# Summing the edge weights of an attention aggregation on VectorE instead of TensorE, in a two-layer graph network on one core

## The reference, cut to what matters

```
h = (x @ W1).reshape(N, 4, 512)
e = leaky_relu(as_n[src] + ad_n[dst], 0.2)          # one score per edge and head
ex = exp(e - segment_max(e, dst)[dst])
denom = segment_sum(ex, dst)                        # <- the sum that the change moves
alpha = ex / (denom[dst] + 1e-16)
out = segment_sum(alpha[:, :, None] * h[src], dst)  # 1250 x 4 x 512
h = elu(out + b1)
```

## Time and profile before

| | |
|---|---|
| median of 3 runs | 2060.86 us (2059.75 to 2064.29) |
| the profiled execution | 2063.02 us, its span 2061.2 us |
| the stage `aggregate_layer1`, first to last product | 1389 to 1719.6 us |
| PE busy, whole span | 1849.1 us, 90% |
| DVE busy, whole span | 1466.7 us, 71% |
| mean granted TensorE clock | 0.955 |

### The profile page before, as it was taken

One profiled execution on the slowest core, in us unless ns is written; L12 is line 12 of the kernel. 1 busy time (PEld: TensorE's weight loads), 2 busy tenths in 40 slices (PEclk: granted clock), 3 DMA queues, 4 the chain that ended last, 5 costly groups with the idle time before them and its releaser, 6 DMA issues. The chain is left out here.

```text
span 2061.2 us, 29930 instructions
## 1 busy us (share of the span) xinstructions
PE 1849.1 (90%) x11272; PEld 1758.3 (85%) x11272; DVE 1466.7 (71%) x2541; ACT 960.7 (47%) x1465; POOL 141.4 (7%) x129
## 2 busy tenths in 40 slices
PE   5998999993999999986999599969999995999898
PEld 4666779993999999985999479969999995999798
DVE  6887849996989988955555328728888885235666
ACT  1222222214888898864211222227788775232633
POOL 5000122110000000000110101200000000000000
PEclk9999999996999999997999799989999998999999
DMA  3111144435284445518543485454433404645402
GB/s 117 50 54 50 39 150 140 112 94 139 67 200 97 106 93 133 139 19 230 164 140 119 142 243 174 142 151 113 144 95 94 135 33 135 180 104 130 120 1 75
DMA packets 183967, 240.11 MB, mean 116 GB/s; under 512 B 76347, under 2 KB 155283, under 8 KB 183586
## 3 DMA queue, kind: packets, MB, share of 16 engines
q1 hardware_dynamic: 175852, 210.73, 37.2%
q0 software_dynamic: 7216, 24.91, 4.1%
q10 hardware_dynamic: 768, 2.70, 0.5%
HBM read 169.43 MB, written 68.86 MB: 116 GB/s over the span
## 5 line engine op out<-in xcount | busy, mean ns | idle before, releaser
L966 PE MATMUL p_o<-h_in,p 125*125 125x193 f32 x2400 | 399.1, 328 | 25.2 <-DVE p L925 20.9
L966 PEld LDWEIGHTS p_o<-h_in,p 125*125 125x125 f32 x2400 | 393.1, 188 | 28.2 <-DMA h_in<-h_rows 21.1
L882 ACT ACTIVATE e<-uv,col 125x1250 f32<-125x1250 f32 x240 | 299.2, 1346 | 18.1 <-DMA uv<-uv_rows 14.9
L1522 PE MATMUL p_o<-p_hi,h_parts 125*128 125x416 f32 (+1 forms) x960 | 282.5, 355 | 25.7 <-DVE p_lo L1456 19.4
L1522 PEld LDWEIGHTS p_o<-p_hi,h_parts 125*128 125x128 f32 x960 | 181.5, 189 | 31.9 <-issue 19.6
L920 DVE TENSOR_TENSOR e<-e 125x1250 f32<-125x1250 f32 x120 | 174.2, 1452 | 30.5 <-ACT e L882 30.4
L647 DVE CUSTOM_DVE_ANT_0 max_junk<-src_row,G 125x1250 bf16<-125x1250 f32 x120 | 180.9, 1574 | 10.6 <-DMA src_row<-score_rows 9.9
L734 PE MATMUL p_h<-pw_hi,x1T 128*125 128x384 f32 x720 | 186.0, 339 | 0.0
L925 DVE SCALAR_TENSOR_TENSOR p<-e,CT 125x1250 f32<-125x1250 f32 x120 | 175.3, 1461 | 4.1
L1259 PE MATMUL p_h<-pw_hi,x2T 128*125 128x256 f32 x960 | 175.8, 285 | 0.0
L1522 PE MATMUL p_o<-p_lo,h_parts 125*128 125x416 f32 (+1 forms) x480 | 169.7, 354 | 0.0
(11 more groups left out here) (236 smaller groups left out, 3469.1 us busy)
## 6 DMA issues: line engine op xcount, KB each, us to landing
f_raw<-turned SPq DMA_DIRECT2D x40, 500.0 KB
h_rows<-h_out SPq DMA_DIRECT2D x32, 560.0 KB
h_parts<-h_rows SPq DMA_DIRECT2D x40, 448.0 KB
uv<-uv_rows SPq DMA_DIRECT2D x24, 546.9 KB
turned<-out_f SPq DMA_DIRECT2D x18, 625.0 KB
G<-turned SPq DMA_DIRECT2D x20, 562.5 KB
h_rows<-h_out SPq DMA_DIRECT2D x24, 424.4 KB
h_in<-h_rows SPq DMA_DIRECT2D x24, 424.4 KB
```

The source lines that it names most:

```text
L882: last = a.activation(e[:, g % RING, kind, :], uv[:, hh, kind, :], ACT.Exp, bias=col_src[kind][:, bass.ds(i * 2 + hh, 1), s])
L966: last = nc.tensor.matmul(p_o[:, b, n * 256:n * 256 + C0 + 1], p[:, g % RING, d * T:(d + 1) * T], h_in[:, hh, s, 0:C0 + 1], start=(s == 0 ...
L1522: last = nc.tensor.matmul(p_o[:, bank(n, c), 0:w], h[:, s, kind, cols].bitcast(F32R), pp[:, g % RING, 0:w], start=(s == 0 and j == 0), sto ...
```

## The change

DVE adds the weights `p` of the ten steps of a third into one tile `acc` (two tiles of 418 columns, used in turn), nine additions for each third. The two products with ones in every step go. In their place PE makes one product for each third, of `ones_f` and `acc`, both plain fp32 rather than fp32r, after the second chunk of step 9; only this product needs the fifth bank. ACT no longer makes the rounded copy of `ones`. ACT's exponentials wait, beside `p_split`, for the addition that read the ring slot (`added`).

```
         p_lo = sb("p_lo", [T, RING, W], F32R)
         ones_f = sb("ones_f", [T, 128], F32)
-        ones = sb("ones", [T, 128], F32R)
+        acc = sb("acc", [T, 2, W], F32)
...
-            act.wait_ge(ones_set, 1)
-            a.activation(ones[:], ones_f[:], ACT.Copy).then_inc(ones_set, 1)
...
                 if g >= RING:
                     act.wait_ge(p_split, g - RING + 1)
+                    m, step = divmod(g - RING, NT)
+                    act.wait_ge(added, m * (NT - 1) + max(step, 1))
...
+            def add(n, s, low, before):
+                if s == 1 and n >= 2:
+                    dve.wait_ge(summed, n - 1)
+                if s > 1:
+                    dve.wait_ge(added, n * (NT - 1) + s - 1)
+                dve.wait_ge(p_ready, n * NT + s + 1)
+                v.tensor_tensor(acc[:, n % 2, 0:low.shape[1]], low, before, ALU.add).then_inc(added, 1)
+
             for g in range(STEPS_ALL):
...
                 v.scalar_tensor_tensor(low, low, 1.0, CT[:, s, at:at + w], ALU.min, ALU.mult).then_inc(p_ready, 1)
+                if s == 1:
+                    add(n, s, low, e[:, (g - 1) % RING, 0, 0:w])
+                elif s:
+                    add(n, s, low, acc[:, n % 2, 0:w])
                 if g:
                     rest_of_p(g - 1)
...
-            def sum_weights(g, n, s, w):
-                if s == 0:
-                    bank_is_free(n, CW)
-                for pp in (p_hi, p_lo):
-                    last = nc.tensor.matmul(p_o[:, bank(n, CW), 0:w], ones[:], pp[:, g % RING, 0:w],
-                                            start=(s == 0 and pp is p_hi), stop=(s == NT - 1 and pp is p_lo))
-                if s == NT - 1:
-                    last.then_inc(summed, 1)
-                return last
+            def sum_weights(n):
+                w = THIRDS[n % 3][1]
+                bank_is_free(n, CW)
+                pe.wait_ge(added, (n + 1) * (NT - 1))
+                nc.tensor.matmul(p_o[:, bank(n, CW), 0:w], ones_f[:], acc[:, n % 2, 0:w], start=True, stop=True).then_inc(summed, 1)
...
                 pe.wait_ge(p_split, g + 1)
-                if s:
-                    sum_weights(g, n, s, w)
                 for c in range(CW):
...
-                if s == 0:
-                    last = sum_weights(g, n, s, w)
+                    if s == NT - 1 and c == 1:
+                        sum_weights(n)
                 last.then_inc(p_used, 1)
```

More of the change, by code:

```diff
@@ L1312, in aggregate_layer1 @@
         p_used = sem("p_used")
+        added = sem("added")
         summed = sem("summed")
@@ L1486, in _ @@
         def _(pe):
-            pe.wait_ge(ones_set, 2)
+            pe.wait_ge(ones_set, 1)
             def bank_is_free(n, c):
```

## The result

The changed kernel takes 2098.09 us, the median of 4 runs (2091.59 to 2104.50), the kernel before 2062.57 (4 runs, 2059.75 to 2064.39). The ratio is 1.0173, with a 95% interval of 1.0139 to 1.0208: slower, clear of the noise. 2092 us was forecast, with 2084 to 2101.

The account below looks back on a forecast made before the run. The loop of DVE and ACT was taken as the bound, PE close behind. Paid additions +31 us, first end +1, last end -1: 2063.0 + 31 = 2094, less 2.2 for the median, 2092 us; range 2084 to 2101.

Parts of the forecast that it names:

- The bound: In each middle third, the loop of DVE and ACT sets the 27.53 us pace; PE is second, needing 26.7 us.
- Four free, five paid: Of nine additions a third, steps 4 to 7 hide in DVE's waits for ACT; five cost 3.1 us.
- The price of an addition: On DVE, each addition costs 0.62 us net, one dependence; bounds 0.51 and 0.73 us.
- The rule weighed: Skill's rule for DVE: every instruction waits for the pipe to empty, semaphores cost nothing extra; an addition would cost 0.51 us.
- Rival 2: On DVE, an addition costs the bare 0.51 us spacing: +25.5 us, 2086 us in all; chance 8%.
- The first end: Up to DVE's first taking of the sums, at 1416.4 instead of 1415.23: +1 us (0 to +2).
- The last end: From eleventh to last taking of the sums, where DVE waits for PE: 26.1 us against 26.97, so -1 us.
- this term of the sum: PE's one plain fp32 product of 416 columns per third costs 0.34 us, from the spacing of fp32 transposes.
- The upper bound: For the last third, with the lower clock and the fp32 product at 1.15 us: +0.2 us.
- rival 3: PE's clock stays at 1.2 GHz, 0.29 us a product, 35 us a third: +91 us, 2152 us; chance 3%.
- rival 4: PE paces the third and additions are hidden: 24.5 us a third, -36 us, 2025 us; chance 3%.
- The 2.2 us taken off for the median: Whole kernel: the median of the runs lies 2.2 us below the profiled execution, taking 2094 to 2092 us.

Follow-up runs that it names:

- e5: Changed kernel with all additions left out, PE's one product per third reading a tile of constant ones: 27.53 us a third, span 2059.9 us.
- e9: Kernel before with ACT's twelve ELU operations two to a step in steps 4 to 9: 27.0 us a third, median 2057.32 us, ratio 0.9980.
- e11: Changed kernel with all nine additions behind p_lo, one wait each, and ELU operations two to a step in steps 4 to 9: 28.51 us a third, 2076.04 us.
- e1: Changed kernel with only the additions of steps 4, 5, 6 and 7 of each third kept: 27.53 us a third, span 2059.1 us.
- e2: Changed kernel with only the additions of steps 1, 2, 3, 8 and 9 of each third kept: 31.01 us a third, span 2088.2 us.
- e4_onewait: Changed kernel with the additions of steps 2 to 9 waiting on one semaphore instead of two: 30.73 us a third.
- e3_late: Changed kernel with each addition placed behind the p_lo of its step instead of directly behind the weight: 30.04 us a third, 2088.5 us.
- e6: Kernel before with the nine additions put into DVE and PE's twenty products with ones kept: 30.9 to 31.3 us a third, span 2098.9 us.
- e7_pool: Changed kernel with the nine additions of a third made by GpSimd instead of VectorE: 30.5 to 30.8 us a third, ratio 1.0165 to the kernel before.

## Why the prediction was right, and where it was off

*The bound.* Right. The loop of DVE and ACT paces a third: e5 takes PE's cost away and gains nothing, e9 shortens DVE's waits for ACT from 3.3 to 1.4 us a third and gains 0.5 us until DVE waits for PE's sums; in e11 DVE has no wait left and a third is its bare need, 28.51 us. That need is 24.0 + 9 x 0.50: the 24.3 of the prediction was 0.3 too high, since a printed wait is some 0.09 us less than the whole gap (the maximum behind an ELU operation starts 0.65 us behind it after the wait is taken off, and 0.56 without a wait). The forecast's sum did not use it.

*Four free, five paid.* Right, and shown apart by e1 and e2.

*The price of an addition.* The step that was off. I took 0.62 us, one dependence; it was 0.69 to 0.70, since eight and, from the third third on, all nine of a third's additions wait on two semaphores. The surplus of 0.07 over five paid additions and ten thirds is 3.5 us of the 3.8 that the middle was too low. e4_onewait takes most of it away, 30.73 for 31.00. It lay inside the bound of 0.73, for a reason that I had not named. The text of the change showed both waits; I priced only the one that blocks.

*The rule weighed.* By the Trainium skill, VectorE: DVE Perf Modes, section The DRAIN you can't avoid, each instruction waits for the pipe to empty and a semaphore costs nothing extra; the section adds that an instruction that is not held starts earlier. Of the semaphore this kernel shows something else: 0.50, 0.63 and 0.70 us for one addition with no dependence ahead, with one, and with one and a second wait. Rival 2, built on it, would have been 30.08 us a third; the changed kernel has 31.00.

*The first end.* +2.0 instead of +1. DVE took the sums at 1417.22, 0.8 us later than the 1416.4 worked out. 0.6 is a later start of DVE (1386.56 against 1385.96), whose exponentials waited for a DMA; the ten second waits ahead of the first taking are worth up to 0.7, more than the rest; how much of that went into the early waits was not worked out.

*The last end.* +0.6 instead of -1. PE in the last third (timeline; then windows with PEclk behind POOL's busy time), which answers to the earlier trace rows:

```profile
1731.32 0.71 PE L1529 MATMUL p_o<-p_hi,h_parts 125*128 125x416 f32 x1 [4.53 <-DVE z L1445]
...
1753.94 0.86 PE L1515 MATMUL p_o<-acc,ones_f 125*128 125x416 f32 x2
1754.32 0.67 PE L1529 MATMUL p_o<-p_hi,h_parts 125*128 125x416 f32 x1
1754.82 0.35 PE L1529 MATMUL p_o<-p_lo,h_parts 125*128 125x416 f32 x1
```

```profile
1731.40:1736.80 5.40, 5.40 (x16) 5.15 (x17) 5.12 (x10) 5.27 (x11) 0.00 (x0) 0.50 0.00 0
1737.00:1742.00 5.00, 5.00 (x28) 4.94 (x28) 4.48 (x9) 4.90 (x10) 0.00 (x0) 1.00 0.12 43
```

The fp32 product is two instructions and holds the next product back to 1754.82, so it costs 1754.82 - 0.19 - 1753.94 = 0.69 us, not the 0.34 read off the transposes: this term of the sum was half its size. The 105 products ahead of it take 1753.94 - 1731.32 = 22.6 us, where 20.1 + 1.4 = 21.5 were forecast, 1.1 us more. The granted clock was 0.50 for 5.5 us behind the stop, not 3.4, which by (5.5 - 3.4) / 2 is that 1.1. Together 0.35 + 1.1 is the 1.5 us between the 26.1 worked out and the 27.57 measured. The upper bound, 26.1 + 0.8 for a product of 1.15 us, is 26.9 and so -0.1, not the +0.2 of the prediction, and +0.6 lies outside either.

How long the low clock lasts is not fixed by the stop. e2_five has the same products behind the eleventh taking and a longer stop, 5.68 us; its granted clock was 0.50 for only 3 us of work, and its last distance is 26.40. In e4_onewait it is 26.76, in e3_late 27.42. So the product's 0.35 comes in every such kernel, and the 1.1 of the clock differs between 0 and about 1 from one profile to the next. No run changed the clock alone.

The Trainium skill, FP8 and Floating Point Precision, section TensorE Precision Notes, gives true FP32 four passes, 0.76 us by the estimate in the prediction: the measured 0.69 is near it, and twice what the spacing of the transposes gave.

*The clock as a bound (rival 3).* It did not become one: DVE waits for PE's sums only at the very end. The granted clock is 0.90 in the mean over the ten distances, where it was 1.00, since it fell to 0.50 in PE's long stops, and in the middle PE had room for that. The rival's price of the low clock was too small: 16 products took 5.40 us at 0.50, 0.34 each and not 0.29, so a third wholly at that clock would need some 41 us, an estimate. The Trainium skill, TensorE: Matmul & The Clock Gate, section HAM oscillation, describes loops whose clock falls anew in each iteration, and the trace agrees: behind each of the ten stops of 4.4 to 5.9 us the granted clock was 0.50, for about 3 to 6 us of work.

*The faster case (rival 4)* is excluded by e5 and e6.

*What came out right by luck.* The sum for the profiled execution was 6.4 us too low in the stage (3.8 in the middle, 1.6 at the last end, 1.0 at the first). What follows the stage was 1.6 us shorter for no reason that the prediction names, so 4.8 remained. The 2.2 us taken off for the median was too much as well: the changed kernel's median is 0.75 below its profiled execution, and the kernel before's, with its fourth run, 0.45 below. The forecast held because its range was wide enough for all of this.

*Open:* the -1.6 us behind the stage. Its instructions are the same, and from the last taking to the end the profiles of all these kernels range from 342.1 (e3_late) to 344.3 us (e11_all_dve), with 343.7 before and 342.2 in the changed kernel.

## What to carry to other kernels

Before moving work from a busy engine to a less busy one, take the stage's period apart: whose waits for whom are in it, and how much work stands between two of them. Work that lands ahead of a wait is free up to the wait's size, and work that lands behind the last wait is paid in full, even on an engine that looks 87% busy beside one at 98%. What pays is to even out the needs, and to put a dependent instruction one place later.

## What was not expected of the hardware

A GpSimd addition of 125 x 416 fp32 beside VectorE's two-operand instructions lengthened some of these, a maximum from 0.58 to 1.47 us (e7_pool): an idle GpSimd was no free place for it. A second semaphore wait ahead of a VectorE instruction is an instruction of its own and costs 0.07 us where the first wait is for the instruction just ahead (the changed kernel against e4_onewait), and nothing where both are long fulfilled (e3_late). Behind a stop of 5.7 us the granted clock was 0.50 for 3 us of work (e2_five), behind one of 4.5 us for 5.5 (the changed kernel).
